# Eight layer norms on one core: their moments taken by the stages ahead, one affine norm moved into ScalarE's copy, and 32 gathered rows in flight where 8 were

## The reference

```python
def _layernorm(x, axis=-1, eps=1e-05):
    m = jnp.mean(x, axis=axis, keepdims=True)
    v = jnp.var(x, axis=axis, keepdims=True)
    return (x - m) / jnp.sqrt(v + eps)
...
x = x + layer(_layernorm(x))
```

## Time and profile before

| what | us |
|---|---|
| median of 3 runs (lowest to highest) | 4460.46 (4452.94 to 4465.13) |
| the profiled execution | 4451.35 |
| its span in the profile | 4449.6 |
| PE busy | 3893.6 (88%) |
| PEld busy | 2419.6 (54%) |
| DVE busy | 2324.5 (52%) |
| ACT busy | 1724.7 (39%) |
| POOL busy | 1224.0 (28%) |

### The profile page before, as it was taken

One profiled execution on the slowest core, in us unless ns is written; L12 is line 12 of the kernel. 1 busy time (PEld: TensorE's weight loads), 2 busy tenths in 40 slices (PEclk: granted clock), 3 DMA queues, 4 the chain that ended last, 5 costly groups with the idle time before them and its releaser, 6 DMA issues. The chain is left out here.

```text
span 4449.6 us, 105359 instructions
## 1 busy us (share of the span) xinstructions
PE 3893.6 (88%) x45357; PEld 2419.6 (54%) x45424; DVE 2324.5 (52%) x4313; ACT 1724.7 (39%) x2719; POOL 1224.0 (28%) x1771
## 2 busy tenths in 40 slices
PE   6888769999995686799899769999999999999879
PEld 3333555555543373477655546665666665666646
DVE  4764244454456124444433247777667777677642
ACT  2345212122112010455211145656655566655532
POOL 2000120000002405321000045555554555554512
PEclk9999759999996797899899889999999999999889
DMA  1000000000003062100100000000000000000000
GB/s 51 1 1 1 30 0 27 11 1 11 11 1 110 31 191 68 41 1 1 58 0 1 6 11 9 9 9 11 10 10 9 10 9 9 9 9 9 6 15 20
DMA packets 39404, 92.00 MB, mean 21 GB/s; under 512 B 7534, under 2 KB 27791, under 8 KB 35562
## 3 DMA queue, kind: packets, MB, share of 16 engines
q1 hardware_dynamic: 28586, 69.54, 4.7%
q0 software_dynamic: 6144, 11.62, 0.9%
q10 hardware_dynamic: 4224, 4.19, 0.3%
HBM read 70.05 MB, written 20.45 MB: 20 GB/s over the span
## 5 line engine op out<-in xcount | busy, mean ns | idle before, releaser
L2713 PE MATMUL ps<-h_normT,h_w 128*128 128x512 f32 (+1 forms) x1008 | 423.7, 525 | 27.3 <-DVE h_xx L3300 20.3
L3234 DVE SCALAR_TENSOR_TENSOR h_cv<-h_raw,h_cw,h_cv 128x1023 f32<-128x1023 f32 (+2 forms) x288 | 391.8, 1370 | 19.7 <-ACT h_cv L3061 18.7
L3378 DVE SCALAR_TENSOR_TENSOR h_st<-h_st,d_gcs,ps 128x64 f32<-128x64 f32 x448 | 123.4, 276 | 341.9 <-PE ps L3009 341.8
L3060 ACT ACTIVATE h_raw<-ps 128x512 f32<-128x512 f32 x192 | 114.1, 594 | 401.1 <-PE ps L2713 400.3
L2713 PEld LDWEIGHTS ps<-h_normT,h_w 128*128 128x128 f32 x1008 | 164.9, 189 | 132.3 <-issue 114.6
L460 ACT ACTIVATE a_prob<-ps 128x1024 f32<-128x1024 f32 (+1 forms) x192 | 154.6, 811 | 192.7 <-PE ps L372 104.4
L944 PE MATMUL ps<-a_probT,a_v 128*128 128x512 f32 x512 | 227.8, 604 | 0.9 <-DVE a_probT L1082 0.9
L2610 POOL TENSOR_TENSOR h_gm<-h_gm,h_tmp 128x15 f32<-128x15 f32 (+7 forms) x480 | 214.7, 447 | 37.6
L2175 PE MATMUL ps<-h_normT,e_wgu 128*128 128x512 f32 (+1 forms) x448 | 203.3, 597 | 3.6 <-DMA e_wd<-in_e_wd 2.4
L1231 POOL MEMSET r_zero<- 128x2048 f32 x1 | 1.8, 1805 | 727.5 <-POOLq L54 727.5
L3009 PEld LDWEIGHTS ps<-h_st,h_mT 64*64 64x64 f32 x1792 | 90.0, 132 | 198.3 <-issue 194.1
(11 more groups left out here) (537 smaller groups left out, 9334.0 us busy)
## 6 DMA issues: line engine op xcount, KB each, us to landing
m_wgu<-in_m_wgu SPq DMA_DIRECT2D x8, 1408.0 KB
h_w<-in_d_w SPq DMA_DIRECT2D x48, 128.0 KB
m_wd<-in_m_wd SPq DMA_DIRECT2D x8, 704.0 KB
m_rows_in<-r_zero SPq DMA_DIRECT2D x4, 1024.0 KB
e_xe<-m_rows_in SPq DMA_DIRECT2D x8, 512.0 KB
m_rows_out<-e_y ACTq DMA_DIRECT2D x8, 512.0 KB
e_wgu<-in_e_wgu SPq DMA_DIRECT2D x1, 3520.0 KB
a_t_raw<-in_t_w SPq DMA_DIRECT2D x4, 768.0 KB
```

The lines of the kernel that those rows point to most:

```text
L2713: last = pe.matmul(ps[:, PROJ[m], lo:hi], w[:, kind, k, :], hT[:, k, b * S + tb * BANK + lo:b * S + tb * BANK + hi], start=(k == 0), stop= ...
L3234: dve.scalar_tensor_tensor(out=d, in0=raw[:, kind, 0:S - back], scalar=tap(pr, kind, TAPS3 - 1 - back), in1=d, op0=ALU.mult, op1=ALU.add). ...
```

## The change

It has three parts.

**Moments.** `x_stats` is kept for the whole program, and `measure(core, dve, t)` is the `bn_stats` of tile t. The stage that makes the last addition to a tile of `x_resid` now also takes its moments, on DVE, after waiting for the add's semaphore. `layer_norm` begins with `bn_aggr`. At the program's start `x` is loaded in four transfers of four tiles, and DVE takes the moments of each as it lands. In thought0 and attention3 they stand between and behind the adds; in combine1 after the first row of the next tile; in mixer2 two tiles behind the adds.

**Affine norm.** In n2 weight and bias are loaded as columns of the transposed layout and applied by ACT in its copy: 16 activations 128x256 (two for each pair of tiles) with a per-partition scale and bias, where 8 copies of 128x512 were. DVE's 32 multiplications and additions go.

**Combine.** `RING` is 32. DVE's order is written out: the products of gate and up stand earlier between the rows, and the shared adds go pair by pair with the rows of a tile between. Every row add now waits for the one ahead, across tiles too.

```diff
+        self.stats = sb("x_stats", [P, NT, 6])
         self.ps = es.enter_context(nc.psum_tensor("ps", [P, 8, BANK], F32))
+
+def measure(core, dve, t):
+    return dve.bn_stats(core.stats[:, t, :], core.x[:, t, :])
...
         @block.sync
         def _(sp):
-            sp.dma_start(core.x[:], core.dram["x"]).then_inc(loaded, 16)
-            sp.wait_ge(loaded, 16)
+            for i in range(PIECES):
+                t0, t1 = piece(i).start, piece(i).stop
+                sp.dma_start(core.x[:, t0:t1, :], core.dram["x"][:, t0:t1, :]).then_inc(loaded[i], 16)
+
+        @block.vector
+        def _(dve):
+            for i in range(PIECES):
+                dve.wait_ge(loaded[i], 16)
+                for t in piece(i):
+                    measure(core, dve, t)
...
             for t in range(NT):
-                dve.bn_stats(stats[:, t, :], core.x[:, t, :]).then_inc(stats_ready, 1)
-            for t in range(NT):
-                dve.wait_ge(stats_ready, t + 1)
-                dve.bn_aggr(mv[:, t, :], stats[:, t, :]).then_inc(mv_ready, 1)
+                dve.bn_aggr(mv[:, t, :], core.stats[:, t, :]).then_inc(mv_ready, 1)
...
                 dve.tensor_tensor(core.x[:, t, :], ps[:, t % 8, 0:H], core.x[:, t, :], ALU.add).then_inc(x_added, 1)
+                if t >= 1:
+                    dve.wait_ge(x_added, t)
+                    measure(core, dve, t - 1)
+            dve.wait_ge(x_added, NT)
+            measure(core, dve, NT - 1)
...
+            for n in range(HALF):
+                dve.wait_ge(x_done, n + 1)
+                measure(core, dve, n)
             finish(1)
+            for n in range(HALF, NT):
+                dve.wait_ge(x_done, n + 1)
+                measure(core, dve, n)
...
-    RING = 8
+    RING = 32
...
                     dve.wait_ge(fetched[n % RING], 16 * (n // RING + 1))
-                    if r >= 1:
+                    if n >= 1:
                         dve.wait_ge(added, n)
-                    elif t >= NT // 2:
+                    if r == 0 and t >= NT // 2:
                         dve.wait_ge(x_added, t - NT // 2 + 1)
                     dve.scalar_tensor_tensor(out=core.x[:, t, :], in0=row[:, n % RING, :], scalar=wv[:, r, t:t + 1],
                                              in1=core.x[:, t, :], op0=ALU.mult, op1=ALU.add).then_inc(added, 1)
-
-            for b, tb in enumerate(blocks):
-                for c in range(SC):
-                    n = b * SC + c
-                    dve.wait_ge(silu_ready, n + 1)
-                    dve.tensor_tensor(hid[0:SM[c], b, c, :], ps[0:SM[c], 2 * (n % 3) + 1, :], silu[0:SM[c], n % 3, :],
-                                      ALU.mult).then_inc(hid_ready, 1)
-                    add_rows(n)
-                for j in range(4):
-                    t = 4 * tb + j
-                    dve.wait_ge(down, 2 * b + j // 2 + 1)
+                    if r == 0 and t >= 1:
+                        measure(core, dve, t - 1)
+
+            def inner(b, c):
+                n = b * SC + c
+                dve.wait_ge(silu_ready, n + 1)
+                dve.tensor_tensor(hid[0:SM[c], b, c, :], ps[0:SM[c], 2 * (n % 3) + 1, :], silu[0:SM[c], n % 3, :],
+                                  ALU.mult).then_inc(hid_ready, 1)
+
+            def add_shared(b, pair):
+                for j in (2 * pair, 2 * pair + 1):
+                    t = 4 * blocks[b] + j
+                    dve.wait_ge(down, 2 * b + pair + 1)
                     dve.scalar_tensor_tensor(out=core.x[:, t, :], in0=ps[:, 6 + j // 2, (j % 2) * H:(j % 2 + 1) * H],
                                              scalar=sgate[:, t:t + 1], in1=core.x[:, t, :], op0=ALU.mult,
                                              op1=ALU.add).then_inc(x_added, 1)
-            for t in range(len(blocks) * SC, NT):
+
...
+            inner(0, 4)
+            add_rows(2)
+            inner(0, 5)
+            add_rows(3)
+            add_shared(0, 0)
+            add_rows(4)
+            add_shared(0, 1)
+            add_rows(5)
+            inner(1, 0)
+            add_rows(6)
+            inner(1, 1)
...
+            add_rows(9)
+            add_shared(1, 0)
+            add_rows(10)
+            add_shared(1, 1)
+            for t in range(11, NT):
                 add_rows(t)
+            dve.wait_ge(added, NT * TOP1)
+            measure(core, dve, NT - 1)
...
-            sp.dma_start(w[:], dram["s2_ln_w"].broadcast_to([P, H])).then_inc(load, 16)
-            sp.dma_start(b[:], dram["s2_ln_b"].broadcast_to([P, H])).then_inc(load, 16)
+            sp.dma_start(w[:], dram["s2_ln_w"]).then_inc(load, 16)
+            sp.dma_start(b[:], dram["s2_ln_b"]).then_inc(load, 16)
...
-            dve.wait_ge(load, 32)
-            for t in range(NT + 2):
-                if t < NT:
-                    dve.wait_ge(x_h, t + 1)
-                    dve.tensor_scalar(h[:, t, :], h[:, t, :], mv[:, t, 0:1], rstd[:, t:t + 1], ALU.subtract,
-                                      ALU.mult).then_inc(centred, 1)
-                if 1 <= t < NT + 1:
-                    dve.wait_ge(centred, t)
-                    dve.tensor_tensor(h[:, t - 1, :], h[:, t - 1, :], w[:], ALU.mult).then_inc(scaled, 1)
-                if t >= 2:
-                    dve.wait_ge(scaled, t - 1)
-                    dve.tensor_tensor(h[:, t - 2, :], h[:, t - 2, :], b[:], ALU.add).then_inc(h_ready, 1)
+            for t in range(NT):
+                dve.wait_ge(x_h, t + 1)
+                dve.tensor_scalar(h[:, t, :], h[:, t, :], mv[:, t, 0:1], rstd[:, t:t + 1], ALU.subtract,
+                                  ALU.mult).then_inc(h_ready, 1)
 
         @block.scalar
         def _(act):
             act.wait_ge(aggr, NT)
             act.activation(std[:], mv[:, :, 1], ACT.Sqrt, bias=core.eps[:, 0:1]).then_inc(std_ready, 1)
+            act.wait_ge(load, 32)
             for u in range(NT // 2):
                 act.wait_ge(turned, u + 1)
-                act.activation(core.hT[:, :, u * 2 * P:(u + 1) * 2 * P],
-                               ps[:, u % 4, :].rearrange("p (k n) -> p k n", k=KC), ACT.Copy).then_inc(copied, 1)
+                for k in range(KC):
+                    last = act.activation(core.hT[:, k, u * 2 * P:(u + 1) * 2 * P], ps[:, u % 4, k * 2 * P:(k + 1) * 2 * P], ACT.Identity,
+                                          bias=b[:, k:k + 1], scale=w[:, k:k + 1])
+                last.then_inc(copied, 1)
...
             def end(t):
                 for g in range(2):
                     gate(t, g)
+                dve.wait_ge(xa, 4 * UNITS3)
                 for k in range(4):
                     add(t, k)
+                    for j in range(2):
+                        measure(core, dve, 2 * k + j)
+                    if k >= 1:
+                        dve.wait_ge(xa, 4 * UNITS3 + k)
+                        for j in range(2):
+                            measure(core, dve, NQ + 2 * k - 2 + j)
+                dve.wait_ge(xa, 4 * UNITS3 + 4)
+                for j in range(2):
+                    measure(core, dve, NT - 2 + j)
```

More of the change, by code:

```diff
@@ L1112, in _ @@
                 dve.tensor_tensor(xs, ps[:, u % 4, :].rearrange("p (t n) -> p t n", t=2), xs, ALU.add).then_inc(x_added, 1)
+                if u >= 1:
+                    dve.wait_ge(x_added, u)
+                    measure(core, dve, 2 * u - 2)
+                    measure(core, dve, 2 * u - 1)
+            dve.wait_ge(x_added, NT // 2)
+            measure(core, dve, NT - 2)
+            measure(core, dve, NT - 1)
 def layout_attention1(a):
@@ L1534, in _ @@
                                              op1=ALU.add).then_inc(x_added, 1)
-            for t in range(len(blocks) * SC, NT):
+            inner(0, 0)
+            inner(0, 1)
+            add_rows(0)
+            inner(0, 2)
+            add_rows(1)
+            inner(0, 3)
+            inner(0, 4)
[9 more added lines that the diff above has]
+            inner(1, 1)
+            inner(1, 2)
+            add_rows(7)
+            inner(1, 3)
+            add_rows(8)
+            inner(1, 4)
+            inner(1, 5)
+            add_rows(9)
[3 more added lines that the diff above has]
+            for t in range(11, NT):
                 add_rows(t)
+            dve.wait_ge(added, NT * TOP1)
+            measure(core, dve, NT - 1)
 def layout_experts1(a):
@@ L1571, in affine_norm2 @@
     with Phase(core, "n2") as ph:
[L1572 removed]
+        w, b = ph.sb("w", [P, KC]), ph.sb("b", [P, KC])
         stats, mv = ph.sb("stats", [P, NT, 6]), ph.sb("mv", [P, NT, 2])
         std, rstd = ph.sb("std", [P, NT]), ph.sb("rstd", [P, NT])
[L1575 to L1576 removed]
+        load, stat, aggr, std_ready, own_dve, x_h, h_ready, turned, copied = (
+            ph.sem(n) for n in ("load", "stat", "aggr", "std", "own_dve", "x_h", "h", "turned", "copied"))
         block = ph.block()
@@ L2013, in residuals @@
             def residuals(i):
+                if i >= 3:
+                    dve.wait_ge(x_added, i - 1)
```

(4 more changed lines are left out.)

19 lines of the change are left out of this document (9 added, 10 removed).

## The result

The changed kernel took 4427.76 us in the median of four runs (4422.84 to 4430.77), the kernel before 4461.24 beside it: a ratio of 0.9933 with a 95% interval of 0.9914 to 0.9952: 33.5 us less by the medians, 29.9 by the ratio. 4430 was forecast, in a range of 4402 to 4447.

A forecast was written before the change was run, and what follows sets the result against it. PE is busy 88%, but phase edges were taken as bound by DVE, and combine1 by PE's late shared down product. Moments 24.85 plus affine norm 9.0 minus combine 3.5 saves 30.3: 4460.5 to 4430 us, range 4402 to 4447.

The forecast's parts named there:

- the term for combine: Combine1: ring and order make the next layer norm start at 1772.7 instead of 1769.26, a loss of 3.5 us.
- The lower bound of 20: Moments over eight layer norms: saving if only attention0's and experts2's tails hid any bn_stats, 20 us against 24.85 forecast.
- What I named as paying in full: thought0 and attention1: DVE has no gaps, so all 16 bn_stats show, and each loses 0.1 us.
- the pause: Combine1: POOL stops at gather 48 instead of 32; PE's post, held until then, comes at about 1724.7, 21 us later.
- three gate-up pieces of the next: Combine1: before its release PE finishes its down block and three pieces, 23 matmuls at 1.04 us; three pieces remain, until 1736.
- The second hold: Combine1: POOL's last 16 gathers land at 1750 and hold the second down block's posts until 1752 to 1760, taken as 1758.
- No stall: Rival, 17%: PE is never held in combine1; the next layer norm starts at 1748.4, 20.9 us gained, total 4406.
- Short stalls: Rival, 17%: each PE stall in combine1 lasts only 4.8 us; combine1 saves 7.8 us, total 4418.
- The stall isn't ended by the pause: Rival, 10%: PE's stall in combine1 lasts 43 us as in route1; 4447 to 4456, no change by measure.
- Slower: Rival, 4%: the 43 us stall hits both down blocks of combine1; 19 us slower, 4479.
- the change wouldn't do what it says: Case, 2%: bn_stats tails or ACT's copies cost all they could; 23 us off, 4437, still faster.
- PE starves of instructions: Combine1 and route1: PE lacks instructions while POOL's transfers run, and a pause frees it; route1 shows 42.7 us of such waits.

The follow-up runs named there:

- a_again_c: The changed kernel without an edit, timed again beside the kernel before in a set with late posts: 4442.41 us, ratio 0.9957.
- a_again: The changed kernel without an edit, beside the kernel before in a set without late posts: 4367.54 us, ratio 0.9891 to before.
- ring16_b: The changed kernel with RING = 16 instead of 32, in a set with late posts: one execution took 4410.15 us.
- ring16_c: The changed kernel with RING = 16 instead of 32, timed in a set with late posts: 4425.38 us, ratio 0.9922 to before.
- ring48_b: The changed kernel with RING = 48 instead of 32, in a set with late posts: one execution took 4449.98 us.
- x0_before: The kernel before, without an edit, run once more: one execution took 4431.35 us, in a set where its median is 4423.9.
- u_affine: The changed kernel with the affine norm of n2 as before, in a set without late posts: 4391.95 us, ratio 0.9933 to before.

## Why the prediction was right, and where it was off

**The sum.** With moments and affine norm as the undone parts show them, and combine as the two first profiles do, the change was worth 23.6 + 9.4 - 10.1 = 22.9 us; these two profiles have 22.6 in all, and 30.3 was forecast. That the median came out 2 us from 4430 is in part luck: the term for combine was 6.6 too good, and the scatter of the runs made up for it. A second comparison at a place with late posts, a_again_c, has 20.6 us by the medians.

**Moments.** Right, and the size too: 24.85 forecast, 23.6 between two profiles without late posts. What I named as paying in full paid in full (thought0, attention1). The lower bound of 20 was added up wrongly: with the tails of mixer2 and attention3 not hidden, the prediction's own terms give 3.8 + 9.0 - 4 x 0.1 + 5.2 = 17.6. That the first pair of profiles shows 7.8 for attention3 is not the change. These are the phase's busy times and granted clock (last but two) from the windows of the changed kernel in the result and in a_again_c, the same code:

```profile
2552.82:4256.20 1703.38, 1579.85 (x34576) 1021.37 (x34608) 1166.81 (x1804) 990.01 (x1572) 888.44 (x1411) 0.96 0.03 9
```

```profile
2550.10:4280.91 1730.81, 1603.05 (x34576) 1037.99 (x34608) 1166.51 (x1804) 991.28 (x1572) 888.45 (x1411) 0.94 0.03 9
```

1703.4 against 1730.8 us, at a granted clock of 0.96 against 0.94, with DVE's busy time the same. In twelve of fourteen profiles the phase lies between 1703 and 1724, and in the other two at 1731. In the four profiles of a_again's set the whole execution varies by 14.2 us and this phase by 13.2: it makes most of the scatter, and its range is wider than any term of my sum.

**Affine norm.** 9.0 forecast, 9.4 measured. A pair of ACT's copies took 1.02, where 1.05 was assumed, and 0.46 each when the pairs stand close; from the end of the first pair to that of the last it is 7.4, as forecast.

**Combine.** At the place where the result was measured the pause did what I said: POOL stops at gather 48, and the first shared add comes 68.0 us after the first gather, where the prediction has 1724.7 - 1658.43 = 66.3. The size was off: the layer norm starts 120.95 after the first gather, not 114.3. The term that was mis-sized is "three gate-up pieces of the next (23 matmuls, at route1's 42.7 / 41 = 1.04 us each)". It doesn't add up by itself: a piece is 8 matmuls and 11 of the down block were left, so that 23 matmuls make one and a half pieces. And 1.04 is the mean of waits that the view lists, not the distance of matmuls. The timeline of before has that distance:

```profile
1480.46 1.01 PE L1159 MATMUL ps<-h_normT,m_sgu 128*128 128x512 f32 x1 [1.79 <-issue]
...
1483.26 1.01 PE L1159 MATMUL ps<-h_normT,m_sgu 128*128 128x512 f32 x1 [1.79 <-issue]
```

2.80 us. From 1706 until the release PE did only the last twelve matmuls of its down block, and no piece of the next. All six pieces came from 1726.23 on, and the second down block ended at 1763.62, 106.4 after the first gather, where 1748 - 1658.43 = 89.6 was forecast: 16.8 late. The second hold, which I had put 10 us beyond that block, didn't come: gathers landed until 1749.7, and the down block began at 1751.62 and took 12.00. So +3.5 became +10.1, by two errors that in part offset each other. With them a piece of the mechanism fell: under those last 16 gathers PE ran 48 matmuls at speed. Flowing gathers alone don't hold PE.

**The rivals.** "No stall" had 17%, and is what happens elsewhere: its combine1 of 90.0 is met within 1.1 us there (90.1 to 91.1), though it gains 10.6 to 13.3 and not 20.9, as the kernel before is shorter there too. The prediction didn't see that the place decides. "Short stalls" (17%) had each stall at 4.8 us, and the first shared add early; it came at 68.0. "The stall isn't ended by the pause" is refuted by how long PE's matmuls come singly: from 1686.96 to 1694.86 with the ring of 16 (ring16_b), 1705.89 to 1722.96 with 32, and 1689.73 to 1742.51 with 48, each time until 1 to 2.3 us after the last landing. "Slower" (4%) needed a second long stall, which no profile has; and that the change wouldn't do what it says (2%) is refuted by its first two parts.

What is left open is why posts are late in one place and not in another, and whether instructions or only the posts and the issue are held. One thing points at PE's supply of instructions. As the first down block of combine1 begins, one packet of 16 KB moves on an instruction queue (columns of the view: packets, MB, share of the DMA engines' time). In the changed kernel it starts at 1695.2; this is the view from 1694 to 1698:

```profile
q8 instruction: 1, 0.02, 1.6%
```

PE slows at 1705.9. The same packet stands at the same place of PE's program in all profiles, in route1 too. In the six profiles with late posts the slow run begins 8.6 to 11.1 us behind it, in route1 and in combine1, twelve times of twelve:

| combine1 of | packet starts | PE slow from | later |
|---|---|---|---|
| before | 1689.0 | 1698.9 | 9.9 |
| after | 1695.2 | 1705.9 | 10.7 |
| a_again_c | 1699.5 | 1710.0 | 10.5 |
| ring16_b | 1675.9 | 1687.0 | 11.1 |
| ring16_c | 1690.4 | 1700.7 | 10.3 |
| ring48_b | 1680.3 | 1689.7 | 9.4 |

That fits the 48 gate-up matmuls ahead of that block, which ran at speed under gathers, and the missing second hold: the next packet of that queue moved at 1779. But where posts aren't late the packet moves in the same place and nothing slows (x0_before at 1666.4, u_affine at 1644.0), and a short slow stretch of before, from 1747.3 on, has none ahead of it. So my words "PE starves of instructions" are a lead that the traces strengthen, not a cause that they show: no run here changed the supply of instructions. The Trainium skill (Runtime: NRT & Kernel Launch, Instruction fetch mechanics) has fetch hidden in straight-line code; that agrees with the sets without late posts (12.00 us a block under the same gathers), and whether it fails in the other sets no run here shows.

## What to carry to other kernels

A deeper ring can cost what it removes: the pause of a full ring may be what lets another engine go on, so ask of a wait what it protects before taking it away, and try a size between. Price a held engine by the distance between its instructions in the timeline, not by the mean of a view of waits. And when a profile shows an engine waiting for a "remote" post or for "issue", run the same kernel elsewhere before costing a change by it: 30 us of route1 and 9 of combine1 were such a place.

## What the runs showed of the hardware that was not expected

- While POOL's indirect transfers flow, PE's posts and the pace of its instructions depend on the place where the program runs: the work of route1 takes 175 to 180 us in some sets and 135 in others, same instructions, and its first down block, under the scatters, 12.00 us only in the latter. It isn't the flow alone: in the slow places too PE runs at speed for 35 us and more under gathers (48 + 36 matmuls by 1705.9 in the changed kernel), and again after a pause.
- Where it happens, PE does one matmul each 1.4 to 3.5 us and posts arrive 5 to 49 us late (49 in route1 of ring16_b). In combine1 the post comes 1 to 5 us after the last transfer before a pause has landed, in route1 up to 7. It isn't bound to the landing: one post of ring48_b came 28 us ahead of it, one of route1 in before 11 us.
- With a ring that never fills and no late posts, POOL's 64 gathers (83 to 84 us) and its drain, which ends 5.3 us after the last of them, bound combine1: 90.1 to 91.1 us, whatever the size from 16 to 48 and the order.
